# Where SyncE's queue carries the repeat of the step sizes' product and the projection's first loads: two moves in the issue order of a fused scan kernel

## The chip, the cores and the metric

One Trainium2 chip, one core of it. The metric is device time in microseconds (us) of one execution of the whole kernel, lower is better. Times are compared as medians of several runs.

## The reference, cut to what matters

The model runs four images of 64x64 positions and 96 channels through two state-space layers and two attention and feed-forward layers. The time goes into the two state-space layers:

```python
# one state-space layer; K = 4 directions, D = 192 channels, N = 16 states, L = 4096
xz = x @ in_proj_w.T;  xi, z = split(xz)
xc = silu(depthwise_conv3x3(xi) + conv_b)
xs = four orders of the same xc            # layer 0: rows, columns, both backwards; layer 1: windows of 1, 2, 4, 8
dts, Bs, Cs = split(einsum(xs, x_proj_w));  delta = softplus(einsum(dts, dt_w) + dt_b)
def step(h, inp):                          # 4096 times
    h = exp(dt_t[..., None] * A) * h + (dt_t * u_t)[..., None] * B_t[:, :, None, :]
    y = einsum('bkdn,bkn->bkd', h, C_t)
y = sum of the four directions' y, each put back in image order, plus Ds * xs
y = layernorm(y) * silu(z);  x = x + y @ out_proj_w.T
```

## The kernel before, in words

There are eight scans (four images times two layers), in the order image 0 layer 0, image 1 layer 0, image 0 layer 1, image 1 layer 1, and the same for images 2 and 3. I number them 0 to 7. A scan has 16 steps (four directions times four stretches of 1024 positions), 128 steps in all. A step has 24 tiles. A tile is 128 partitions (32 channels times 4 states) by 1024 positions, and its work is spread over the engines like this:

- TensorE fills a PSUM slot with B, repeated over partitions (fill, L1071).
- DVE multiplies it by the product of step size and input, which lies in the buffer `dur` (inp, L1572), and runs the recurrence (states, L1587; L1583 for the two tiles of every eight whose input GpSimd prepares, L1707).
- ScalarE makes the decays from the step sizes in the buffer `dtr` (decay, L1336).
- GpSimd multiplies the states by C, which lies in `crep` (product, L1693). The ring of states has three buffers, so scan n of DVE waits until the product n - 3 is done.
- TensorE sums over the states (reduce2, L1084), ScalarE evicts (collect), SyncE stores (store_y, L770).

`dtr`, `dur`, `crep` and `brep` hold each channel's row repeated over partitions. The repeating is done by DMA: load_dt (L753) and load_du (L762) issue two transfers of 512 KB for each group of eight tiles (three groups, g = 0 to 2, in a step), load_c (L739) one for each q = 0 to 3, used from tile 2q of the step on, and load_b (L744) one, used by GpSimd right after the step's first product. Every DMA of the kernel is issued by SyncE, on one queue, in the order of its program. An instruction that waits there holds all that is behind it.

SyncE's loop over the tiles i = 0 to 23 of step w sets that order. At i = 0 come group 1 of `dtr` and `dur` and `crep` q = 2, at i = 2 q = 3, at i = 8 group 2 of `dtr` and `dur`, and for the next step, w + 1, group 0 of `dtr` at i = 18, group 0 of `dur` and `crep` q = 0 at i = 20, `brep` at i = 21 and `crep` q = 1 at i = 22. The product itself, step size times input, is GpSimd's (delta_u, L1684): its first half, the only one that group 0 needs, is made in tile 17 after the tile's own product. load_du waits for it (du_g), and for the scans that still read the buffer (scan_v).

Beside the scan each engine advances a side program by two half tiles (ticks) a tile, with `next(side)`. From the fifteenth tick of scan s on (tick 14, tile 7; LEAD = 14), it is the projection of scan s - 1 (post): eight chunks of 512 positions, started every 39 ticks. A chunk adds up five inputs of 2 x 192 KB each (SUMS: directions 1, 3, 0 and 2 from `y_d`, then the layer's input from `u_d`), on TensorE in ticks s = 0, 2, 4, 8 and 10 of the chunk (L914), normalises, multiplies by the gate z (load at s = 23, product on GpSimd at s = 29, L1659), projects and adds to the image `xb` at s = 38 (L1489). The first chunk's ticks begin 8 ticks after the post's start (X_LEAD). post_load (L612) issues the inputs: the fifth of a chunk at s = 2, the next chunk's four at s = 12, 4, 31 and 37. For layer 0 directions 1 and 3 are read across the columns, in pieces of 8 elements, which makes 6144 pieces of 32 bytes in each transfer. Scans 1, 2, 5 and 6 have such a projection beside them; scans 3, 4 and 7 have one of layer 1, whose loads are all in long rows. load_x (L586) loads the whole image, 1.5 MB, into `xb`. After the post comes the next conv (pre) or an attention layer (attn), each on the same ticks, then nothing.

Of the kernel before, what the change touches and what calls it, by code (L numbers as in the profile page):

```python
# [238 lines left out]
def follow(*sides):  # L239
    for side in sides:  # L240
        yield from side


def build_program(nc, a, out):
# [6 lines left out]
    def dram(name, shape):  # L251
        return nc.dram_tensor(name, shape, F32, kind="Internal").ap()
# [4 lines left out]
    x_d = dram("x_d", [nb, CH, L])  # L257
# [4 lines left out]
    with ctx:  # L262
# [6 lines left out]
        def after(e, s, n):  # L269
            if n > 0:  # L270
                e.wait_ge(s, n)
# [72 lines left out]
        ykt = [v[0:CH, r, :].rearrange("p (h t) -> p h t", h=2) for v in (hs, dec, us) for r in range(3)]  # L344
# [25 lines left out]
        def lane(c, overlapped):  # L370
            return lanes[0 if overlapped else c % LANES]
# [22 lines left out]
        def sum_buffer(m, n, overlapped):  # L394

            if overlapped:
                i = n % 5
                r = i % 4
                return yk[r], yk_in[r], 32 * (2 * m + i // 4 + 1 if r == 0 else m + 1)
            t, r = divmod(n, len(ykt))
            return ykt[r], ykt_in[r], 32 * (t + 1)
# [4 lines left out]
        def chunk(c):  # L411
            return xb[:, 1 + ROWS * c:1 + ROWS * (c + 1), 1:1 + SIDE]

        def rows(v):
            return v.rearrange("p (r w) -> p r w", w=SIDE)
# [62 lines left out]
        def beside(jobs, stages, overlapped):  # L478


            if overlapped:
                for _ in range(LEAD):
                    yield
            for kind, n in jobs:
                yield from stages[kind](n, overlapped)
# [11 lines left out]
        def post_lead(overlapped):  # L497
            return X_LEAD if overlapped else 0

        def post_every(overlapped):  # L500
            return POST_EVERY if overlapped else POST_LANES
# [7 lines left out]
        def post_ticks(overlapped):  # L509
            return post_every(overlapped) * (C8 - 1) + 39  # L510
# [7 lines left out]
        def landed(m, c, one, of_lane, size, overlapped):  # L518


            return (one, size * (m + 1)) if overlapped else (of_lane[c % LANES], size * (c // LANES + 1))
# [17 lines left out]
        def _(sp):  # L539
            n = 0  # L540
# [45 lines left out]
            def load_x(done, src):  # L586
                after(sp, cu_p, C8 * UNITS * done.pre)
                after(sp, x_out, 16 * done.saves)
                after(sp, o_out, 16 * done.outs)
                sp.wait_ge(set_g, 1)  # L590
                sp.dma_start(xb[:, 1:1 + SIDE, 1:1 + SIDE], rows(src)).then_inc(x_in, 16)
# [20 lines left out]
            def post_load(j, n, overlapped):  # L612
                l = order[j][1]
                c, i = divmod(n, 5)
                m = C8 * before["post", j].post + c
                if not overlapped:
                    after(sp, yt_v, (n - len(ykt)) // 5 + 1)
                elif i == 2:
                    after(sp, pg_g, m)
                elif i == 3:  # L620
                    after(sp, pj_p, m)
                else:
                    after(sp, sm_p, 5 * m + (0, -3, 0, 0, 1)[i])
                buf, arrived, _ = sum_buffer(m, n, overlapped)
                for h in range(2):
                    ch = slice(CH * h, CH * (h + 1))
                    k = SUMS[i]
                    if k == K:
                        src, dst = u_d[j][ch, B * c:B * (c + 1)], buf[:, h, :]
                    elif l == 0 and k % 2 == 1:  # L630
                        src = y_d[j, k][ch, :].rearrange("p (w r) -> p w r", r=SIDE)[:, :, ROWS * c:ROWS * (c + 1)]
                        dst = buf[:, h, :].rearrange("p (w r) -> p w r", r=ROWS)
                    else:
                        src, dst = y_d[j, k][ch, B * c:B * (c + 1)], buf[:, h, :]
                    sp.dma_start(dst, src).then_inc(arrived, 16)

            def post(j, overlapped):
                b, l = order[j]
                done = before["post", j]
                sp.wait_ge(y_out, 32 * NG * STEPS * (j + 1))  # L640
                after(sp, uz_out, 32 * C8 * done.pre)
                after(sp, fy_a, C8 * done.attn)
                if not overlapped:
                    sp.wait_ge(scan_v, W * NT)
                    sp.wait_ge(red_p, W * NP)
                after(sp, fx_g, C8 * done.attn)
                for n in range(4 if overlapped else len(ykt)):
                    post_load(j, n, overlapped)
                load_x(done, a["x"][b] if l == 0 else x_d[b])
                for _ in range(post_lead(overlapped)):  # L650
                    yield
                for tick in range(post_ticks(overlapped)):
                    for c in range(C8):
                        s = tick - post_every(overlapped) * c
                        m = C8 * done.post + c
                        if overlapped and s == 2:
                            post_load(j, 5 * c + 4, True)
                        if overlapped and s in (12, 4, 31, 37) and c + 1 < C8:
                            post_load(j, 5 * (c + 1) + (12, 4, 31, 37).index(s), True)
                        if not overlapped and s == 12:  # L660
                            for n in range(5 * c + len(ykt), min(5 * (c + 1) + len(ykt), 5 * C8)):
                                post_load(j, n, False)
                        if s == 23:
                            sp.wait_ge(pv_p, m + 1)
                            arrived, _ = landed(m, c, zq_in, zqt_in, 32, overlapped)
                            for h in range(2):
                                sp.dma_start(lane(c, overlapped).zq[:, h, :], z_d[j][CH * h:CH * (h + 1), B * c:B * (c + 1)]).then_inc(arrived, 16)
                        if s == 38 and done.saved:
                            sp.wait_ge(px_v, m + 1)
                            sp.dma_start(rows(x_d[b])[:, ROWS * c:ROWS * (c + 1), :], chunk(c)).then_inc(x_out, 16)  # L670
                    yield
# [117 lines left out]
            for w in range(W):  # L789
                if w % STEPS == 0:  # L790
                    side = beside(plan[w // STEPS + 1], stages, True)
                    if w == 0:
                        side = follow(head, side)
                if w % STEPS == STEPS - 1:
                    run(side)
                for i in range(NT):
                    if i == 0:
                        load_dt(1, w)
                        load_du(1, w)
                        if w:  # L800
                            load_c(NQ - 2, w)
                    if i == 2:
                        load_c(NQ - 1, w)
                    if i == 1:
                        if w + 1 < W and late(w + 1):
                            load_u(w + 1)
                    if i == 6 and w + 2 < W and not late(w + 2):
                        load_u(w + 2)
                    if i == 4 and w:
                        store_y(2, w - 1)  # L810
                    if i == 8:
                        load_dt(2, w)
                        load_du(2, w)
                    if i == 12:
                        store_y(0, w)
                    if i == 20:
                        store_y(1, w)
                    if w + 1 < W:
                        if i == (8 if late(w + 1) else 0):
                            store_c(0, w + 1)  # L820
                        if i == (13 if late(w + 1) else 10):
                            store_c(1, w + 1)
                        if i == 18:
                            load_dt(0, w + 1)
                        if i == 20:
                            load_du(0, w + 1)
                        if i == 21:
                            load_b(w + 1)
                        if i in (20, 22):
                            load_c((i - 20) // 2, w + 1)  # L830
                    next(side, None)
                    next(side, None)
# [982 lines left out]
```

## Time and profile before

| | |
|---|---|
| median of 3 runs | 11373.29 us (11363.34 to 11389.22) |
| the profiled execution | 11397.64 us, of which span 11395.9 us |
| DVE busy | 10173.2 us (89%) |
| GpSimd (POOL) busy | 9736.9 us (85%) |
| TensorE busy | 8819.1 us (77%) |
| DMA queue of SyncE | 64.3% of 16 engines' span |

The span is that of one profiled execution; its own time lies 24.4 us above the median. The profile gives for each engine its instructions, how long it sat idle before one, and whose work ended that idle time. SyncE's rows show when a DMA was issued and how long SyncE was held by issuing it.

### The profile page before, as it was taken

How to read it: one execution, taken by the hardware profiler on the slowest of the kernel's cores; microseconds unless marked ns; L12 is line 12 of the kernel's file. 1: busy time of each engine (PE TensorE's matmuls, PEld its weight loads, DVE VectorE, ACT ScalarE, POOL GpSimd, SP SyncE). 2: the span in 40 equal slices, each digit the busy share in tenths (PEclk: the TensorE clock that was granted, in tenths of full speed). 3: DMA queues.
4: the chain of work that ended last, by engine and by line, in shares of the span. 5: the costliest groups of instructions: out<-in, count | busy, mean ns of one | idle time of the engine just before them, and what ended most of it. 6: DMA issues, size and time to landing. Idle time of an engine off the chain costs nothing.

```text
span 11395.9 us, 94804 instructions
## 1 busy us (share of the span) xinstructions
PE 8819.1 (77%) x26272; PEld 2206.4 (19%) x26272; DVE 10173.2 (89%) x6087; ACT 6991.9 (61%) x10714; POOL 9736.9 (85%) x4231
## 2 busy tenths in 40 slices
PE   7876677876778777769777787888688876777767
PEld 2211111211112111212112121122111221122213
DVE  4899998999889999989999998899988999999973
ACT  5665555665556556677565765566755666667644
POOL 4899988899888999989988888888988889998860
PEclk9865577865779568769777787788677876777766
DMA  4666689566875566656776668956687566665550
GB/s 113 141 150 132 134 155 157 152 135 142 158 158 151 132 157 162 151 130 148 169 157 152 133 140 157 158 149 137 137 155 161 136 152 142 159 163 120 125 138 11
DMA packets 1779117, 1627.04 MB, mean 143 GB/s; under 512 B 1323598, under 2 KB 1324912, under 8 KB 1778588
## 3 DMA queue, kind: packets, MB, share of 16 engines
q1 hardware_dynamic: 1778588, 1620.97, 64.3%
q8 instruction: 212, 3.47, 0.1%
q14 instruction: 317, 2.60, 0.1%
HBM read 623.22 MB, written 192.15 MB: 72 GB/s over the span
## 4 chain that ended last, share of the span: by engine, by line
DVE 24%; issue 22%; PE 19%; POOL 18%; ACT 8%; DMA 4%; SPq 3%; DVEq 0%; POOLq 0%; ACTq 0%
POOL pr L1693 13%; DVE hs L1587 10%; DVE ps L1572 9%; DVE hs L1583 4%; PE ps L1084 3%; PE ps L1071 3%; PE ps L879 2%; PE ps L914 2%; PE ps L1062 2%; DMA dur<-us 2%; ACT dec L1336 2%; POOL dur L1707 2%; POOL bup L1707 2%; PE ps L1046 2%; POOL us L1684 1%
## 5 line engine op out<-in xcount | busy, mean ns | idle before, releaser
L1693 POOL TENSOR_TENSOR pr<-hs,crep 128x1024 f32<-128x1024 f32 x3072 | 7184.6, 2355 | 1175.9 <-DVE hs L1587 510.9
L1587 DVE TENSOR_TENSOR_SCAN hs<-dec,carry,ps 128x1024 f32<-128x1024 f32 x1728 | 4054.6, 2346 | 237.6 <-POOL pr L1693 13.4
L1071 PE MATMUL ps<-sbc,selb 96*128 96x512 bf16 x4608 | 1844.0, 492 | 1921.3 <-DVE hs L1587 1310.8
L1572 DVE TENSOR_TENSOR ps<-ps,dur 128x1024 f32<-128x1024 f32 x2304 | 2789.2, 1211 | 436.0 <-PE ps L1071 233.0
L1336 ACT ACTIVATE dec<-dtr,ac 128x1024 f32<-128x1024 f32 x2304 | 2611.0, 1137 | 486.5 <-DVE hs L1587 459.0
L1084 PE MATMUL ps<-pr,red 128*32 128x512 f32 x12288 | 2287.5, 827 | 19.7 <-POOL pr L1693 13.3
L1343 ACT ACTIVATE carry<-hs 128x1 f32<-128x1 f32 x2304 | 457.1, 199 | 2452.5 <-DVE hs L1587 2282.9
L1587 DVE TENSOR_TENSOR_SCAN hs<-dec,zero,ps 128x1024 f32<-128x1024 f32 x576 | 1351.5, 2346 | 72.2 <-ACT dec L1336 1.4
L879 PE MATMUL ps<-xb,tapw 96*96 96x512 f32 x2304 | 1176.8, 632 | 31.1 <-ACT sd L1168 28.5
L1071 PEld LDWEIGHTS ps<-sbc,selb 96*128 96x128 bf16 x4608 | 374.5, 108 | 4058.9 <-DVE hs L1587 2412.3
L1336 ACT ACTIVATE ps<-dtr,ac 128x1024 f32<-128x1024 f32 x768 | 848.6, 1105 | 421.8 <-DVE hs L1587 421.6
L1707 POOL TENSOR_TENSOR dur<-dur,brep 128x1024 f32<-128x1024 f32 x384 | 907.5, 2363 | 2.5 <-DVE ps L1572 2.3
L1707 POOL TENSOR_TENSOR bup<-dur,brep 128x1024 f32<-128x1024 f32 x384 | 905.4, 2358 | 2.3 <-DMA brep<-bc_d 2.3
L1062 PE MATMUL ps<-xdf,tapw 6*96 6x512 f32 x1024 | 777.9, 849 | 50.7 <-ACT de L1311 26.4
L1046 PE MATMUL ps<-us,xp 96*102 96x512 f32 x1024 | 687.6, 808 | 46.1 <-ACT us L1289 24.8
L1583 DVE TENSOR_TENSOR_SCAN hs<-ps,carry,bup 128x1024 f32<-128x1024 f32 x288 | 671.2, 2331 | 57.9 <-issue 30.9
L1684 POOL TENSOR_TENSOR us<-us,de 96x1024 f32<-96x1024 f32 x256 | 603.1, 2356 | 125.3 <-ACT de L1320 125.3
L1583 DVE TENSOR_TENSOR_SCAN hs<-ps,carry,dur 128x1024 f32<-128x1024 f32 x288 | 670.4, 2328 | 13.9 <-ACT ps L1336 7.8
L914 PE MATMUL ps<-sd,eye 96*96 96x512 f32 x896 | 610.0, 799 | 5.2 <-DMA sd<-y_d 3.2
L1084 PEld LDWEIGHTS ps<-pr,red 128*32 128x32 f32 x12288 | 276.7, 124 | 1164.7 <-issue 889.4
L879 PEld LDWEIGHTS ps<-xb,tapw 96*96 96x96 f32 x2304 | 356.6, 169 | 743.4 <-issue 677.7
L1303 ACT ACTIVATE sbc<-ps 96x512 bf16<-96x512 f32 x768 | 443.7, 578 | 16.1 <-PE ps L1052 16.1
(228 smaller groups left out, 7622.2 us busy)
## 6 DMA issues: line engine op xcount, KB each, us to landing
dtr<-de SPq DMA_DIRECT2D x768, 512.0 KB, 8.1
dur<-us SPq DMA_DIRECT2D x768, 512.0 KB, 7.9
crep<-bc_d SPq DMA_DIRECT2D x512, 512.0 KB, 7.3
ust<-u_d SPq DMA_DIRECT2D x256, 384.0 KB, 6.1
y_d<-yst SPq DMA_DIRECT2D x768, 128.0 KB, 2.4
sd<-y_d SPq DMA_DIRECT2D x448, 192.0 KB, 4.6
brep<-bc_d SPq DMA_DIRECT2D x128, 512.0 KB, 7.2
u_d<-sd SPq DMA_DIRECT2D x64, 384.0 KB, 3.1
```

Of the source, the lines that this page charges most:

```text
L879: mm = pe.matmul(bank, tap[:, t, h * CH:(h + 1) * CH], xb[:, c * ROWS + t // 3:c * ROWS + t // 3 + ROWS, t % 3:t % 3 + SIDE], start=(t == ...
L914: mm = pe.matmul(ps[0:CH, bank + h, :], eye[:, :] if k < K else dg[:, l, h, :], v, start=(i == 0), stop=(i == K))
L1046: mm = pe.matmul(ps[0:XROWS, PB, :], xp[:, l, h, k, :], us[:, half(h, w), B * hf:B * (hf + 1)], start=(h == 0), stop=(h == 1))
L1062: pe.matmul(ps[0:CH, PB, :], dtw[:, order[s][1], k, h * CH:(h + 1) * CH], xdf[XD:XROWS, :], start=True, stop=True, tile_position=(XD, 0)). ...
L1071: mm = pe.matmul(ps[:, SLOT + 2 * (n % RS) + hf, :], selb[:, i % GT // 2, :], sbc[:, w % 2, B * hf:B * (hf + 1)], start=True, stop=True)
L1084: mm = pe.matmul(ps[32 * strip:32 * strip + 32, YB, :], red[:, :], pr[:, (2 * m + j) % RP, B * hf:B * (hf + 1)], start=(q == 0), stop=(q = ...
L1336: act.activation(to, dtr[:, 2 * (G % 2) + i % 2, :], ACT.Exp, scale=ac[:, order[s][1], k, i:i + 1]).then_inc(exp_a, 1)
L1572: dve.tensor_tensor(slot(n), slot(n), dur[:, 2 * (G % 2) + i % 2, :], ALU.mult).then_inc(bu_v, 1)
L1583: dve.tensor_tensor_scan(hs[:, n % RH, :], slot(n), bup[:, :] if i % 2 else dur[:, 2 * (G % 2), :], init, ALU.mult, ALU.add).then_inc(scan ...
L1587: dve.tensor_tensor_scan(hs[:, n % RH, :], dec[:, others(n) % RD, :], slot(n), init, ALU.mult, ALU.add).then_inc(scan_v, 1)
L1693: pool.tensor_tensor(pr[:, n % RP, :], hs[:, n % RH, :], crep[:, q, :], ALU.mult).then_inc(prod_g, 1)
L1707: pool.tensor_tensor(to, v, brep[:, :], ALU.mult).then_inc(bup_g, 1)
```

## The change

Three edits in SyncE's program; no other engine's program and no computation changes.

1. load_du(0, w + 1), the repeat of the product for the next step's first group, is issued at i = 18, right behind load_dt(0, w + 1), instead of at i = 20. The side program's ticks 36 to 39 and store_y(1, w) stood between the two places.
2. In the overlapped post the first chunk's four sum inputs (eight DMAs) are no longer issued all at the post's start. They go out in its ticks 0, 2, 4 and 6, so in tiles 7, 8, 9 and 10 of the scan's first step; the group 2 loads of `dtr` and `dur` at i = 8 come between the first and the second.
3. The image's load of the overlapped post moves from right behind those eight to tick 16 behind the lead of 8, which is tick 38 of the step, tile 19: behind load_dt(0), load_du(0), ahead of store_y(1), load_c(0), load_b and load_c(1).

The last post, which runs after all scans, keeps its order.

```diff
-                for n in range(4 if overlapped else len(ykt)):
-                    post_load(j, n, overlapped)
-                load_x(done, a["x"][b] if l == 0 else x_d[b])
-                for _ in range(post_lead(overlapped)):
+                if not overlapped:
+                    for n in range(len(ykt)):
+                        post_load(j, n, False)
+                    load_x(done, a["x"][b] if l == 0 else x_d[b])
+                for tick in range(post_lead(overlapped)):
+                    if tick % 2 == 0:
+                        post_load(j, tick // 2, True)
                     yield
                 for tick in range(post_ticks(overlapped)):
                     for c in range(C8):
...
                         if overlapped and s == 2:
                             post_load(j, 5 * c + 4, True)
+                        if overlapped and tick == 16 and c == 0:
+                            load_x(done, a["x"][b] if l == 0 else x_d[b])
...
                         if i == 18:
                             load_dt(0, w + 1)
-                        if i == 20:
                             load_du(0, w + 1)
```

## Rows read from the trace of the kernel before

**Rows 1.** The page, busy us, share of the span and count of each engine

```profile
PE 8819.1 (77%) x26272; PEld 2206.4 (19%) x26272; DVE 10173.2 (89%) x6087; ACT 6991.9 (61%) x10714; POOL 9736.9 (85%) x4231
```

**Rows 2.** Windows: us, busy of PE, PEld, DVE, ACT, POOL, granted clock, DMA share, GB/s

```profile
650.00:1370.00 720.00, 485.55 (x1398) 83.40 (x1397) 696.29 (x386) 404.15 (x590) 681.21 (x294) 0.58 0.63 137
1470.00:1545.00 75.00, 54.15 (x157) 12.35 (x155) 62.26 (x37) 41.66 (x64) 61.67 (x27) 0.75 1.00 141
1713.00:1810.00 97.00, 76.08 (x217) 17.37 (x215) 78.03 (x45) 49.84 (x55) 81.68 (x36) 0.79 0.94 150
```

**Rows 3.** Waits over the whole span: total us, times, longest

```profile
DVE ps L1572 <- DMA dur<-us: 201.2, 29, 101.6
...
POOL pr L1693 <- DMA crep<-bc_d: 46.7, 6, 10.3
```

**Rows 4.** Timeline of DVE, five waits for dur: start, us, [idle before]

```profile
1508.10 1.23 DVE L1572 TENSOR_TENSOR ps<-ps,dur 128x1024 f32<-128x1024 f32 x1 [3.82 <-DMA dur<-us]
...
1541.51 1.23 DVE L1572 TENSOR_TENSOR ps<-ps,dur 128x1024 f32<-128x1024 f32 x1 [7.19 <-DMA dur<-us]
...
1810.29 1.23 DVE L1572 TENSOR_TENSOR ps<-ps,dur 128x1024 f32<-128x1024 f32 x1 [6.30 <-DMA dur<-us]
...
1900.41 1.23 DVE L1572 TENSOR_TENSOR ps<-ps,dur 128x1024 f32<-128x1024 f32 x1 [2.88 <-DMA dur<-us]
...
7819.75 1.23 DVE L1572 TENSOR_TENSOR ps<-ps,dur 128x1024 f32<-128x1024 f32 x1 [3.29 <-DMA dur<-us]
```

**Rows 5.** Timeline of SyncE, scan 1, step 0: start, us it was held

```profile
1468.56 16.41 SPq L635 DMA_DIRECT2D sd<-y_d  x7
1485.07 0.58 SPq L591 DMA_DIRECT2D xb<-in_x  x1
1485.75 10.92 SPq L753 DMA_DIRECT2D dtr<-de  x2
...
1532.53 1.26 SPq L762 DMA_DIRECT2D dur<-us  x2
1533.88 3.83 SPq L739 DMA_DIRECT2D crep<-bc_d  x1
```

**Rows 6.** Issues of crep: first the one of 1533.88, then that of 1828.05

```profile
DMA to landing us min/median/max: 9.4/9.4/9.4
...
DMA to landing us min/median/max: 7.1/7.1/7.1
```

**Rows 7.** Timeline of SyncE and POOL in a step with nothing beside it

```profile
889.58 1.26 SPq L762 DMA_DIRECT2D dur<-us  x2
...
886.49 2.35 POOL L1684 TENSOR_TENSOR us<-us,de 96x1024 f32<-96x1024 f32 x1
```

**Rows 8.** Timeline, scan 1, step 1: POOL's first product, DVE's eighth scan

```profile
1546.26 2.35 POOL L1693 TENSOR_TENSOR pr<-hs,crep 128x1024 f32<-128x1024 f32 x1 [6.56 <-DVE hs L1587]
...
1568.70 2.32 DVE L1583 TENSOR_TENSOR_SCAN hs<-ps,carry,bup 128x1024 f32<-128x1024 f32 x1
```

**Rows 9.** Timeline, scan 1, step 4: SyncE's third crep, POOL's fifth to seventh product

```profile
1828.05 1.74 SPq L739 DMA_DIRECT2D crep<-bc_d  x1
...
1835.28 6.97 POOL L1693 TENSOR_TENSOR pr<-hs,crep 128x1024 f32<-128x1024 f32 x3 [5.70 <-issue]
```

**Rows 10.** Timeline, scan 3, steps 0 and 1: SyncE's crep, POOL's product

```profile
4214.85 3.84 SPq L739 DMA_DIRECT2D crep<-bc_d  x1
...
4230.54 1.67 SPq L739 DMA_DIRECT2D crep<-bc_d  x1
...
4246.87 9.30 POOL L1693 TENSOR_TENSOR pr<-hs,crep 128x1024 f32<-128x1024 f32 x4
```

**Rows 11.** Timeline, scan 3, step 3: input load, delta_u, its user on PE

```profile
4456.23 2.84 SPq L635 DMA_DIRECT2D sd<-u_d  x2
...
4460.22 2.36 POOL L1684 TENSOR_TENSOR us<-us,de 96x1024 f32<-96x1024 f32 x1
...
4468.40 1.96 PE L914 MATMUL ps<-sd,dg 96*96 96x512 f32 x4
```

## The prediction

> **What bounds the kernel now.** I read the page first: DVE is busy 89% of the span and GpSimd 85% [rows 1]. The windows say where the rest is lost. With nothing beside the scan DVE works 696.3 of 720 us and the DMA engines are busy 0.63 of the time; in the first step of scan 1, where the projection starts, DVE works 62.3 of 75 us and the DMA share is 1.00, and it is 0.94 in step 3 [rows 2]. Of DVE's waits 201.2 us are for `dur`, in 29 waits; the one of 101.6 is the start of the kernel, so 99.6 us in 28 waits can be at stake [rows 3]. They are not spread evenly. I sorted all of them by step, and one wait of each kind stands as an example [rows 4]:
> - first step of scans 1, 2, 5 and 6, the ones with a layer-0 projection: 3.82 before tile 16 and 7.19 before the next step; over the four scans such pairs come to 11.0, 11.0, 9.7 and 11.2, in all 42.9 us;
> - the end of step 3 of the same scans, 6.30 and three like it, together 21.6;
> - the end of step 4, 2.88 and three like it, 12.4;
> - the end of step 10 of scans 5 and 6, 3.29 and 3.64, 6.9;
> - some ten of 0.7 to 2.8 us, mostly the end of step 2, the rest.
>
> SyncE's own timeline tells why. At 1468.56 seven of the eight sum loads hold it for 16.41 us, then comes the image, and the next transfer (dtr, two DMAs) holds it for 10.92; the loads of group 0 for the next step go out only at 1532.53 [rows 5]. An issue costs 0.6 us when the queue is short (1.26 for two there), so the long ones are the queue being full. The image thus occupies it for some 10.3 us (10.92 less one issue of 0.6).
>
> **Part 1, the earlier dur.** In a quiet step it changes nothing: dur goes out at 889.58 while the product it carries is finished at 886.49 + 2.35 = 888.84 [rows 7]. The gain is 0.7 us of lead that nobody waits for. So about 90 of 128 steps are unmoved. Where the queue is full, the two transfers swap places with what stood between, but the work in the queue is the same. What comes after dur (`crep` q = 0, `brep`, q = 1, the next dtr and dur, q = 2) lands no sooner. So the next limit is GpSimd's `crep`, and I price each kind by it.
>
> End of step 3 (21.6 us of DVE waits): nothing comes back. In that case q = 2 goes out at 1828.05 and lands 7.1 later, at 1835.2 [rows 6, 9]; GpSimd, which has waited 5.70 for it, starts its fifth product at 1835.28 [rows 9], and the ring of three lets DVE's eighth scan go only behind that product. DVE would start its step 6.3 earlier and lose it eight tiles later. The input loads that now stand behind dur put about 1 us of transfer into the full stretch. Bounds: -1.5 to +6 a step; I take -1, since the limiting landing is in the trace. Four steps: -4.
>
> End of step 4 (12.4 us): no crep wait follows, so most comes back. The bound below is 0 (a column load behind dur goes out later and pushes `crep`), above 12.4. I take 8. End of step 10 (6.9 us): dtr is stuck behind an image load, dur can follow it at once; bounds 3 and 6.9, I take 6. The scattered ones are followed in scans 1, 2, 5 and 6 by a crep wait of about 10 us, of which the longest is 10.3 [rows 3], so I take 1 for them together, between 0 and 12.
>
> **Part 2, the spread loads.** With one pair of column loads ahead of dtr and dur of group 2 instead of eight DMAs and the image, these go out in tile 8 and, 9.4 us or less from issue to landing like the crep of rows 6, are there long before tile 16. The 3.82 goes. The sum loads now land when their users are due within about a microsecond; I charge 0.4 a scan.
>
> The 7.19 before the next step goes only in part. All that stood ahead of `crep` q = 0 still does, the image included, and the queue is full from 1468 to 1545 [rows 2], so q = 0 lands at 1533.88 + 9.4 = 1543.3 [rows 5, 6] as before, or a little sooner. GpSimd, which started at 1546.26 after DVE's wait [rows 8], can start then: 3.0 us, which is the bound below. DVE may be three tiles ahead of it, though, so its loss is less. From 1543.3 GpSimd needs five products and two inputs at 2.35 each, 16.5 us, to 1559.8; that releases DVE's eighth scan, which began at 1568.70 [rows 8]. That is 8.9, against 11.0 if all comes back. Less 0.4, 8.5 in each of the four scans: +34, with 12 and 43 as ends.
>
> The image moves into the end of step 0 of scans 3, 4 and 7 too, where no wait for dur stood. There it puts 10.3 us ahead of `crep`. q = 0 went out at 4214.85 and would land around 4224; q = 2 went out at 4230.54, and lands near 4238.5, while its product starts at 4246.87 [rows 10]: 8.4 us in hand. Ten more eat that, and GpSimd's first products start 2 to 4 us late. Ends 0 and 6 us a scan, I take 2.5: -7.5. The Trainium skill, page DMA: Bandwidth & Descriptors, section Anatomy of one DMA, would put such a transfer at 2.0 us plus its bytes by 436 GB/s, 5.6 us for 1.5 MB as an estimate; the trace disagrees with its 10.3 of queue, and by the page's price these 7.5 us would be nearly nothing and the sum about 11334.
>
> **The new wait.** At i = 18 SyncE now stands until the product is made. Behind it are the side ticks 36 to 39 and the store of y. The store's buffer is wanted seven tiles later, so it hides. In step 2 or 3 of a projection the tick holds the fifth input. In scan 3 it went out at 4456.23; the product ends at 4460.22 + 2.36 = 4462.6, so it goes out near 4463.9 and lands behind dur, about 4472, while TensorE wants it at 4468.40 [rows 11]. TensorE stands 3 us, DVE's next fill is due 4 to 6 us later, so 0 to 3 of it shows; 1 for each of three scans, -3. The conv's stores at those ticks delay ScalarE by up to 2 us in some four places: -2, between 0 and -6. Gate loads go out later too, but their product on GpSimd is 10 us away: 0.
>
> **Sum.** 34 - 4 + 8 + 6 + 1 - 7.5 - 3 - 2 = 32.5 us. Against the profiled execution that is 11397.64 - 32.5 = 11365; it lies 24.4 above the median, so for the median 11373.29 - 32.5 = 11341 us. A measurement can tell 0.2% from no change, 23 us here.
>
> **Rivals.**
> 1. *The full queue gives it all back.* The DMA share of 0.94 to 1.00 in the stretches at stake [rows 2] and the landing that pins DVE [rows 9] speak for it. Then the first steps give only GpSimd's 3.0 each, 12; the end of step 4 gives 4 and of step 10 gives 3; and -4, -7.5, -3 and -2 stay: 2.5 us, so 11371. By the Trainium skill, page DMA: Bandwidth & Descriptors, section Queues, rings and completion order, transfers of one issuing engine share one ring on each of the same DMA engines and are consumed in ring order, so reordering makes no room; the trace agrees as far as its share of 1.00 goes.
> 2. *Everything waited for comes back.* If shorter column bursts also let `crep` land sooner, all 99.6 us of DVE's waits go, and 11274 is reached. Against it: POOL's 46.7 us of waits for crep [rows 3] lie right behind them.
> 3. *Slower: the image pushes `crep` off.* Its 10.3 us now stand between dur and q = 0 in seven first steps. It decides where GpSimd has less in hand than that. In scans 3, 4 and 7, 8.4 us are in hand for q = 2 but only 1 or 2 for q = 0; if DVE pays 8 in each, 24 are lost. If in the other four q = 0 also lands later than 1543.3, by 5 us, 3 us of loss each takes the place of the 8.5 gained, -12. With 4 and 3 gained at steps 4 and 10 and -4 for step 3, -3 and -2, that is 38 us more, 11411; half of it gives 11392.
>
> **How the numbers follow.** Forecast 0.53, rival 1 0.29, rival 2 0.10, rival 3 0.08. The forecast's own range is 11318 to 11362, from the ends of its largest term (12 or 43 in place of 34) and a few us of the others. Eight in ten: down to 11295, which leaves most of rival 2 out, and up to 11386, which takes in rival 1 and part of rival 3. Faster by over 0.2% means under 11350.5: about 0.46 of the forecast's 0.53, rival 2, and 0.05 of rival 1, 0.61. Slower by over 0.2% means over 11396: 0.05. Between them 0.34.
>
> **What would show it.** In the changed trace DVE's waits for `dur` beside layer-0 projections are gone or below 1 us; if they are not, dur is late for its product. GpSimd's waits for `crep` grow from 46.7 us to about 80, above all at q = 0 of step 1; if they don't, rival 2 holds. Step 0 of scan 1 is 8 to 9 us shorter than before, and step 3 as long as before, 97 us (the window of rows 2). In scan 3 the fifth product of step 1 starts 2 to 3 us later against its step's first tile. I am wrong if the gain of step 3 is kept, if the image's 10.3 us costs nothing in scans 3, 4 and 7, or if the steps with nothing beside them change in length.

## The result, and the profile after

The changed kernel takes 11412.5 us (median of 5 runs, 11410.21 to 11451.97) against 11371.33 for the kernel before (5 runs, 11363.34 to 11389.22): ratio 1.0043 [1.003, 1.0056], so it is slower by 0.43%. Measured a second time it came out at 1.0032 [1.0019, 1.0044]. The forecast was 11341. The two profiled executions differ less, 11397.64 and 11411.21 us, because the one of before lies 26 us above its median. The two profiles of the changed kernel differ by 20 us, so step lengths below are compared as sums over several steps, where possible from two profiles of each kernel.

In the changed kernel load_du is L767, load_dt L758, load_c L744, load_b L749, store_y L775, GpSimd's product L1697, DVE's inp L1576.

The page of the changed kernel, busy us of each engine, answers to [rows 1]: as busy as before.

```profile
PE 8871.1 (78%) x26272; PEld 2220.9 (19%) x26272; DVE 10173.8 (89%) x6087; ACT 6994.2 (61%) x10714; POOL 9742.8 (85%) x4231
```

Its windows, the same stretches as in [rows 2] (us, busy of PE, PEld, DVE, ACT, POOL, granted clock, DMA share, GB/s):

```profile
650.00:1370.00 720.00, 488.03 (x1399) 83.53 (x1398) 696.31 (x387) 404.38 (x590) 681.50 (x295) 0.57 0.62 137
1470.00:1545.00 75.00, 58.16 (x166) 12.98 (x169) 68.83 (x41) 46.10 (x71) 61.97 (x27) 0.70 0.90 124
1713.00:1810.00 97.00, 79.87 (x218) 18.82 (x217) 81.23 (x48) 50.34 (x55) 80.22 (x36) 0.74 0.93 149
```

The quiet stretch is the same (DVE 696.3 in both). In the first step of scan 1 DVE works 68.8 of 75 us in place of 62.3, as wanted, and GpSimd no more than before.

Its waits (total us, times, longest) answer to [rows 3]:

```profile
DVE ps L1576 <- DMA dur<-us: 111.1, 7, 101.5
...
POOL pr L1697 <- DMA crep<-bc_d: 76.1, 10, 10.1
...
ACT sd L1172 <- DMA z_d<-sd: 55.1, 13, 6.9
```

DVE's waits for `dur` are nearly gone: less the start of the kernel, 9.6 us are left of 99.6, most of it 1.5 to 2.2 us at the end of step 0 of scans 1, 2, 5 and 6. GpSimd's for `crep` grew from 46.7 to 76.1 (62.8 in the second profile). The third line is one that the prediction never listed: ScalarE waits until a conv store to `z_d` has left its buffer, 18.0 us in 8 waits before, 55.1 in 13 now.

Where the time went, by steps. A step's length is the time from DVE's first product with `dur` in it to that in the next, added up over the scans named. "Before" is the mean of two profiles, of the kernel before and of the experiment e8, which differs from it in step 7 alone (for step 7 only the kernel before is taken); "changed" is the mean of its two profiles. Two profiles of one kernel differ by up to 6.2 us in the first row and by 4.4 in the others with steps 3 or 4, but by 0.1 in step 7 of the changed kernel. So -3.5 can't be told from nothing, and +18.4 can.

| steps | before | changed | difference |
|---|---|---|---|
| 0 and 1 of scans 1, 2, 5, 6 | 705.3 | 701.8 | -3.5 |
| 3 and 4 of scans 1, 2, 5, 6 | 741.7 | 732.2 | -9.5 |
| 5 of scans 1, 2, 5, 6 | 334.4 | 339.7 | +5.3 |
| **7 of scans 1, 2, 5, 6** | 350.9 | 369.4 | **+18.4** |
| 0 and 1 of scans 3, 4, 7 | 485.2 | 492.5 | +7.2 |
| 2 of scans 3, 4, 7 | 258.8 | 250.7 | -8.1 |
| 3 of scans 3, 4, 7 | 250.2 | 257.0 | +6.8 |
| 11 and 12 of scans 3, 4, 7 | 521.5 | 532.2 | +10.7 |
| all others, by step and group of scans none over 3.4 | | | +9.3 |
| sum | | | +36.6 |

So the gains are small, and a loss stands in places where no wait for `dur` had been.

**Step 7** (steps are numbered from 0). SyncE and then ScalarE in step 7 of scan 1, kernel before (start, us, [idle before]):

```profile
2144.63 0.32 SPq L608 DMA_DIRECT2D u_d<-sd  x1
2145.00 0.45 SPq L609 DMA_DIRECT2D z_d<-sd  x1
...
2149.86 1.25 SPq L762 DMA_DIRECT2D dur<-us  x2
...
2154.30 0.68 ACT L1168 ACTIVATE sd<-ps,cb 96x512 f32<-96x512 f32 x1 [1.54 <-PE ps L879]
```

The same in the changed kernel, with DVE's scan that waits for ScalarE:

```profile
2140.64 1.19 SPq L767 DMA_DIRECT2D dur<-us  x2
2141.87 3.94 SPq L608 DMA_DIRECT2D u_d<-sd  x1
2145.86 2.28 SPq L609 DMA_DIRECT2D z_d<-sd  x1
...
2153.61 0.68 ACT L1172 ACTIVATE sd<-ps,cb 96x512 f32<-96x512 f32 x1 [6.88 <-DMA z_d<-sd]
...
2155.34 2.35 DVE L1587 TENSOR_TENSOR_SCAN hs<-ps,carry,bup 128x1024 f32<-128x1024 f32 x1 [3.90 <-ACT ps L1340]
```

And the time from issue to landing of the store to `z_d`, before:

```profile
DMA to landing us min/median/max: 3.9/3.9/3.9
```

and changed:

```profile
DMA to landing us min/median/max: 7.7/7.7/7.7
```

Counted from the first product of step 7 (2070.4 before, 2064.7 changed), the store to `u_d` is issued at 74.2 and at 77.1: that is the wait for the product. Its issue then holds SyncE 3.9 us in place of 0.3, and the store to `z_d` lands 7.7 after its issue in place of 3.9, with the megabyte of `dur` and the other store ahead of it in the queue. It lands at 78.5 before and at 88.8 now. ScalarE's next eviction into that buffer stands 6.88 us, the decays behind it come late, and DVE stands 3.90. All four scans show it: 4.6 us longer each in the first profile, to 0.1.

### The profile page after: what moved, and what is told of

Read it like the earlier page. It is cut to its first block and busy times, and to the rows that moved or that the text cites. A ratio compares the mean times of both kernels' runs of the same rounds, so it can differ in the third digit from the quotient of the medians.

```text
span 11409.4 us, 94804 instructions
## 1 busy us (share of the span) xinstructions
PE 8871.1 (78%) x26272; PEld 2220.9 (19%) x26272; DVE 10173.8 (89%) x6087; ACT 6994.2 (61%) x10714; POOL 9742.8 (85%) x4231
## 5 line engine op out<-in xcount | busy, mean ns | idle before, releaser
L1697 POOL TENSOR_TENSOR pr<-hs,crep 128x1024 f32<-128x1024 f32 x3072 | 7187.3, 2356 | 1193.1 <-DVE hs L1591 500.4
L1576 DVE TENSOR_TENSOR ps<-ps,dur 128x1024 f32<-128x1024 f32 x2304 | 2787.8, 1210 | 382.4 <-PE ps L1075 269.2
```

The costliest lines, as they stand in the source:

```text
L1576: dve.tensor_tensor(slot(n), slot(n), dur[:, 2 * (G % 2) + i % 2, :], ALU.mult).then_inc(bu_v, 1)
L1697: pool.tensor_tensor(pr[:, n % RP, :], hs[:, n % RH, :], crep[:, q, :], ALU.mult).then_inc(prod_g, 1)
```

## The experiments

Step lengths are in us. Each group of four ran on one chip with the kernel before beside it. The first group asks which part does what.

**e1_dur18**: part 1 alone, the loads as before.

```diff
                         if i == 18:
                             load_dt(0, w + 1)
-                        if i == 20:
                             load_du(0, w + 1)
```

> Part 1 alone: dur for the next step goes out in the nineteenth tile, the projection's loads and the image stay in one burst as before. Theory A (the new wait for the product holds SyncE, and with it the side program's ticks 36 to 39: fifth sum input in step 3, conv stores in step 7): slower than before by 25 to 50 us, and step 7 of scans 1, 2, 5 and 6 about 4.6 us longer, as in the changed kernel. Theory B (the image ahead of crep is what costs): this kernel is faster than before by 10 to 30 us. Theory C (the DMA queue is full, order changes nothing): within 10 us of before.

Measured: 1.002 [1.001, 1.003]. Steps 0 and 1 of scans 1, 2, 5, 6 take 692.7 (705.3 before), steps 3 and 4 take 730.3 (741.7), but step 7 takes 369.9 (350.9) and step 3 of scans 3, 4, 7 257.6 (250.2). Part 1 is a loss by itself, 21 us by the medians, less than the 25 to 50 of theory A. In the first steps it gives 12.6 of the 34 us that were forecast there, more than both parts together. DVE's waits for `dur` in steps 0 and 1 of the four scans are 39.5 us there, hardly less than the 42.9 of before.

**e2_spread_image_late**: part 2 alone, with `dur` in tile 20.

```diff
                         if i == 18:
                             load_dt(0, w + 1)
+                        if i == 20:
                             load_du(0, w + 1)
```

(against the changed kernel)

> Part 2 alone: sum loads spread, image in tile 19, dur in tile 20 as before. Theory A: 15 to 35 us faster than before, since step 0 of scans 1, 2, 5 and 6 still gets 5 us shorter and nothing is held. Theory B: slower than before by 10 us or more, since the image now stands ahead of dur too (it is issued in tile 19, dur in tile 20). Theory C: within 10 us.

Measured: 1.0048 [1.0035, 1.0061], the highest ratio of all, as theory B had it. SyncE and DVE at the end of step 0 of scan 1:

```profile
1517.64 4.03 SPq L591 DMA_DIRECT2D xb<-in_x  x1
1521.71 12.43 SPq L775 DMA_DIRECT2D y_d<-yst  x2
1534.24 1.26 SPq L767 DMA_DIRECT2D dur<-us  x2
...
1543.42 1.23 DVE L1577 TENSOR_TENSOR ps<-ps,dur 128x1024 f32<-128x1024 f32 x1 [13.78 <-DMA dur<-us]
```

The image holds the next issue, the y store, for 12.43 us; `dur` goes out behind both and DVE stands 13.78. Step 0 becomes 5 to 8 us longer in scans 1, 2, 5, 6 and 5 to 11 in 3, 4 and 7. In the changed kernel `dur` is ahead of the image and escapes this; what is behind does not.

**e3_spread_image_early**: the loads spread, the image in half tile 7 of the lead, `dur` in tile 20.

```diff
-                for n in range(4 if overlapped else len(ykt)):
-                    post_load(j, n, overlapped)
-                load_x(done, a["x"][b] if l == 0 else x_d[b])
-                for _ in range(post_lead(overlapped)):
+                for tick in range(post_lead(overlapped)):
+                    if tick % 2 == 0:
+                        post_load(j, tick // 2, True)
+                    if tick == 7:
+                        load_x(done, a["x"][b] if l == 0 else x_d[b])
                     yield
```

> Sum loads spread over the opening half tiles, but the image right behind them (half tile 7 of the lead, tile 10) and dur in tile 20 as before. Only the burst is undone. Theory A and theory B both: faster than before by 15 us (the 3.8 to 5.2 us wait of group 2 in four scans), crep q = 0 not later than before. Theory C: within 5 us of before, the wait returns as a longer one before the next step.

Measured: 0.9992 [0.9983, 1.0]. Step 0 stays as it was, 358.7 against 359.1 over the four scans. DVE's two waits of [rows 4] in scan 1 are now

```profile
1502.13 1.23 DVE L1577 TENSOR_TENSOR ps<-ps,dur 128x1024 f32<-128x1024 f32 x1 [3.86 <-PE ps L1076]
...
1535.40 1.23 DVE L1577 TENSOR_TENSOR ps<-ps,dur 128x1024 f32<-128x1024 f32 x1 [7.06 <-DMA dur<-us]
```

The one before tile 16 (3.82 for `dur`) has only changed its name: `dur` is there and DVE stands 3.86 for TensorE's fill. The one before the next step is as it was (7.19). The expected gain of 15 us in step 0 did not come. So it is in every kernel with the loads spread: in step 0 of the four scans DVE waits 15.7 to 20.8 us for TensorE's fill, and 0 to 4.2 in those with the loads in one burst.

**e4_dur20**: `dur` stays in tile 20, but goes ahead of the y store.

```diff
                     if i == 20:
+                        if w + 1 < W:
+                            load_du(0, w + 1)
                         store_y(1, w)
...
-                        if i == 20:
-                            load_du(0, w + 1)
```

> dur for the next step stays in tile 20 but goes ahead of the store of y instead of behind it: it passes only the two stores, and no side tick is held (the product is done by then). Theory A: faster than before by 5 to 20 us, step 7 of scans 1, 2, 5, 6 as before. Theory B: the same, 10 to 30 us faster. Theory C: within 5 us of before.

Measured: 0.9986 [0.9977, 0.9996]. In step 7 of scan 1 (SyncE, then ScalarE) the conv's stores go first and ScalarE waits for TensorE, not for a store:

```profile
2131.78 0.32 SPq L608 DMA_DIRECT2D u_d<-sd  x1
2132.14 0.45 SPq L609 DMA_DIRECT2D z_d<-sd  x1
2133.79 1.21 SPq L762 DMA_DIRECT2D dur<-us  x2
...
2156.76 0.69 ACT L1168 ACTIVATE sd<-ps,cb 96x512 f32<-96x512 f32 x1 [0.96 <-PE ps L879]
```

Step 7 takes 349.4 over the four scans, step 3 of scans 3, 4, 7 takes 250.1, as before; steps 3 and 4 of the four scans take 733.0 (741.7). The loss is gone and more than half of the gain kept. In step 7 the early place had bought no lead at all: `dur` is issued 72.7 to 76.3 us into the step in the four scans here, and 72.5 to 76.5 in e1, since both wait for the same product. Only what stands behind it differs. In step 3, where the queue is full, e1 is some 4 us earlier (76.4 to 79.2 against 81.5 to 82.9).

The second group tests the account of step 7, the image's place, and whether the parts add.

**e8_dur18_step7_only**: the kernel before, tile 18 in 8 of 128 steps.

```diff
                             load_dt(0, w + 1)
-                        if i == 20:
+                        if i == (18 if w % STEPS == 7 else 20):
                             load_du(0, w + 1)
```

> The kernel before, with the product's repeat in tile 18 in the seventh step of each scan alone (8 of 128 steps), in tile 20 elsewhere. Theory A: step 7 of scans 1, 2, 5 and 6 longer by 4.6 us each, +18 us, ratio 1.0016, with ScalarE waiting up to 7 us for the gate's store; all other steps as before. Rival: the seventh step is long because of what the earlier steps left (the side work shifted), then it stays within 1 us of before and the ratio at 1.000.

Measured: 1.0024 [1.0015, 1.0033]. Step 7 of scans 1, 2, 5, 6 takes 369.7, 18.8 more than before, the others as before. SyncE, ScalarE and DVE in scan 1:

```profile
2139.01 1.19 SPq L762 DMA_DIRECT2D dur<-us  x2
2140.24 3.95 SPq L608 DMA_DIRECT2D u_d<-sd  x1
...
2151.81 0.68 ACT L1168 ACTIVATE sd<-ps,cb 96x512 f32<-96x512 f32 x1 [6.70 <-DMA z_d<-sd]
...
2153.53 2.35 DVE L1583 TENSOR_TENSOR_SCAN hs<-ps,carry,bup 128x1024 f32<-128x1024 f32 x1 [3.73 <-ACT ps L1336]
```

The move in this one step gives the whole pattern, and the rival, that earlier steps leave step 7 long, is out. Its 18.8 us are 0.17%, in the lower part of the measured interval.

**e9_after_image_early**: the changed kernel with the image back in half tile 7 of the lead.

```diff
+                    if tick == 7:
+                        load_x(done, a["x"][b] if l == 0 else x_d[b])
                     yield
...
-                        if overlapped and tick == 16 and c == 0:
-                            load_x(done, a["x"][b] if l == 0 else x_d[b])
```

> The changed kernel with the image back in the lead (half tile 7 of the post), so that part 1 and the spread loads stay and only the image's place is undone. Theory A and B together: parts add, so e1 (1.002) times e3 (0.9992), about 1.001, 35 us under the changed kernel; step 0 of scans 1, 2, 5 and 6 as in the kernel before, step 7 still 4.6 us longer. If the image's place is innocent, it stays at 1.004.

Measured: 1.0015 [1.0006, 1.0024]. Steps 0 and 1 take 693.8 in scans 1, 2, 5, 6 (changed 701.8) and 482.5 in 3, 4, 7 (changed 492.5): 18 us by the late image. The landing of step 1's first `crep` shows it in all seven scans: counted from the start of step 0, q = 0 lands at 91.7 (before), 90.7 (here) and 97.0 us (changed) on average in scans 1, 2, 5 and 6, and at 79.8, 79.3 and 88.9 in 3, 4 and 7. The expectation that step 0 stays as before did not hold: it is 349.9 (359.1), since `dur` in tile 18 shortens it here too.

**e7_after_image_tile23**: the changed kernel with the image in tile 23, behind `crep` q = 0, `brep` and q = 1.

```diff
-                        if overlapped and tick == 16 and c == 0:
+                        if overlapped and tick == 25 and c == 0:
```

> The changed kernel with one thing moved: the image goes out in tile 23 of the first step, behind store_y(1), crep q=0, brep and crep q=1, in place of tile 19. Theory B (the image ahead of the store and of crep takes back what the first steps gained): steps 0 and 1 of scans 1, 2, 5 and 6 together 3 to 6 us shorter than in the changed kernel, those of scans 3, 4 and 7 by 2 to 4, 20 to 30 us in all, so ratio near 1.002; what is left over 1.000 is the wait in tile 18. Theory C: the image only pushes q=2 and q=3 off in place of q=0, and the time stays at 1.004.

Measured: 1.0036 [1.0024, 1.0049], where theory B expected 1.002 and theory C 1.004. SyncE in scan 1:

```profile
1532.65 0.56 SPq L744 DMA_DIRECT2D crep<-bc_d  x1
...
1535.94 0.66 SPq L591 DMA_DIRECT2D xb<-in_x  x1
1536.70 12.67 SPq L758 DMA_DIRECT2D dtr<-de  x2
```

`crep` q = 0 goes out at 1532.65, not 1543.07 (this profile runs 1.2 us ahead there), and steps 0 and 1 of the four scans take 694.2, as with the image early. But the image now holds group 1 of `dtr` for 12.67 us, and in scans 3, 4 and 7 the same two steps take 495.7, 3 more than changed and 13 more than in e9. GpSimd's first product of step 1 is back at its old place there, 5.4 to 6.7 us into the step (9.1 to 10.8 changed), but its fifth, which needs q = 2, starts at 26.3 to 28.0 (25.3 to 26.9 changed, 21.6 to 22.8 before). So theory B came in scans 1, 2, 5 and 6, and theory C in 3, 4 and 7: the image pushes off q = 2 in place of q = 0. It is not the place ahead of q = 0 alone that costs, but the stretch at the turn of the step.

**e6_spread_early_dur20**: e3 and e4 together.

> The two halves that did no harm alone, put together: the four sum loads spread over the lead, the image in half tile 7 of it (ahead of everything of the next step), and the product's repeat in tile 20 but ahead of store_y(1). Theory A (the wait in tile 18 is what costs, the order of the loads gives some us): 0.9992 times 0.9986, about 0.998, some 20 us under the kernel before; the seventh steps of scans 1, 2, 5 and 6 as long as before. Theory C (the queue is full, so no order of it gives anything): within 0.1% of before, and the waits for crep grow by what those for dur lose.

Measured: 0.9992 [0.9983, 1.0001]. Step 7 is as before (349.2). The two small gains do not add.

The third group puts tile 18 only where the first group showed a gain, with the loads in three orders.

**a2_changed_again**: the changed kernel once more.

> The changed kernel itself, on the chip and beside the runs of before of the three below. All theories: the ratio of the first measurement, 1.0043, within its interval of 1.003 to 1.0056.

Measured: 1.0032 [1.0019, 1.0044].

**e10_dur18_steps0to3**: loads as before; `dur` in tile 18 in steps 0 to 3 of scans 1, 2, 5, 6, in tile 20 ahead of the y store elsewhere.

```diff
+            def first_steps(w):
+                return w % STEPS < 4 and w // STEPS in (1, 2, 5, 6)
...
                             load_dt(0, w + 1)
-                        if i == 20:
-                            load_du(0, w + 1)
+                            if first_steps(w):
+                                load_du(0, w + 1)
...
                     if i == 20:
+                        if w + 1 < W and not first_steps(w):
+                            load_du(0, w + 1)
                         store_y(1, w)
```

> Part 1 only where it did good: the product's repeat in tile 18 in steps 0 to 3 of scans 1, 2, 5 and 6, elsewhere in tile 20 ahead of store_y(1); loads of the projection and image as before. Theory A (tile 18 gains in these steps, 14 us in step 3 and about 6 in step 0, and loses in step 7 and in scans 3 and 7): step 7 as before, step 3 of the four scans 14 us shorter together, ratio 0.997 to 0.998, under the 0.9986 of tile 20 everywhere. Rival (what is gained in steps 0 and 3 is given back in steps 1, 4 and 5): 0.9986 or above.

Measured: 1.0 [0.9991, 1.0008]. Step 3 of the four scans takes 366.8 (383.3 before), but step 4 takes 370.1 (358.4): of 16.5 us won, 11.7 come back one step later. The rival named there holds: no gain of tile 18 over tile 20 (e4) shows, even where it shortens a step most.

**e11_steps0to3_spread_early**: the same with the loads of e3.

> The kernel of the run before this with the four sum loads spread over the lead and the image at its half tile 7. If spreading helps once the wait is placed well, another 0.05 to 0.1% under it; if the spread is worth nothing (0.9992 alone, and it added nothing to tile 20), the same within 0.1%.

Measured: 0.9994 [0.9986, 1.0003], the same as e10 within the intervals.

**e12_steps0to3_spread_late**: the same with the loads as changed.

> The changed kernel with tile 18 kept in steps 0 to 3 of scans 1, 2, 5 and 6 alone, so that part 2 stands as changed but the wait is gone from step 7 and the later ones. Theory B (the late image loses by itself, in step 1 of all seven scans and, where dur is in tile 20, in step 0 of scans 3, 4 and 7): 0.2 to 0.4% above the run with the image early, so ratio 1.000 to 1.002. If part 2 only lost through part 1's wait, the same as that run, 0.998.

Measured: 1.0011 [1.0002, 1.002], 0.17% above e11, where 0.2 to 0.4 was expected. Step 0 of scans 3, 4, 7 takes 256.6 (237.6 in e11), since `dur` is in tile 20 there, behind the image:

```profile
4202.80 3.50 SPq L591 DMA_DIRECT2D xb<-x_d  x1
4208.96 9.98 SPq L767 DMA_DIRECT2D dur<-us  x2
...
4227.45 1.23 DVE L1583 TENSOR_TENSOR ps<-ps,dur 128x1024 f32<-128x1024 f32 x1 [5.46 <-DMA dur<-us]
```

Step 7 takes 350.1, so the changed kernel without its wait in the later steps is back from 1.0032 to 1.0011 on the same chip, in spite of these 19 us.

## Why the prediction was wrong

The sign was wrong: 32.5 us of gain were forecast, and 36 to 49 lost (0.32 and 0.43% of 11380). Of the 69 us between forecast and table 30.5 lie in the first steps and 20 in the two terms of the new wait; both steps of the prediction failed, and the first steps are the larger. Rival 3 had the time, 11411, by luck. Its mechanism was seen: it let `crep` q = 0 land 5 us later in scans 1, 2, 5 and 6, and it does so by 5.3 on average. But it put 36 us of loss on that, where the rows of the first steps lose 3.7 net, and 5 on the new wait.

**The new wait, -5, cost 25: this gave the loss.** I priced it at 3 us for the fifth input and "by up to 2 us in some four places: -2, between 0 and -6" for the conv's stores. The stores alone cost 18.4, the fifth input 6.8 (step 3 of scans 3, 4 and 7 takes 254.8 to 261.3 us in the five profiles with tile 18 in every step, 246.3 to 252.9 in the other nine). I had only looked at the wait. In the changed kernel those DMAs also stand behind the two transfers of `dur`, and the store's landing moved by 10.3 us, of which the wait is 2.9, the hold of the store ahead 3.6 and the longer way to landing 3.8. e8 shows the store's part alone, and e4 that nothing of it is left once the side ticks go ahead of `dur`. For the input, SyncE, TensorE and DVE in step 3 of scan 3 of the changed kernel:

```profile
4462.46 1.19 SPq L767 DMA_DIRECT2D dur<-us  x2
4463.69 6.01 SPq L635 DMA_DIRECT2D sd<-u_d  x2
...
4472.98 3.73 PE L918 MATMUL ps<-sd,dg 96*96 96x512 f32 x4 [3.85 <-DMA sd<-u_d]
...
4477.66 1.23 DVE L1576 TENSOR_TENSOR ps<-ps,dur 128x1024 f32<-128x1024 f32 x1 [3.11 <-PE ps L1075]
```

The times were nearly right (the input's issue at 4463.9 and its landing at 4472 foretold, 3 us of waiting on TensorE), but DVE pays 3.11 of the 3.85, where I let 1 show.

A third place was not priced at all: the attention's inputs (`t_d`) on the same ticks in step 12 of scan 7. TensorE waits 7.7 us for them there (8.1 in the second profile), 1.8 before. Step 12 of scan 7 is 96.6 to 97.1 us in the five profiles read that have tile 18 in every step (after, its repeat, e1, e7, e9) and 91.3 to 91.4 in the other nine. Scan 3's step 11 scatters from 91.2 to 101.5 with and without the wait, so of the 10.7 in the table some 5.3 are shown.

**The first steps, +34, gave 3.5: the larger miss.** In steps 0 and 1 of the four scans, as the mean of two profiles of each kernel, DVE's waits for `dur` fell from 43.7 to 9.1 us. But those for TensorE's fill rose from 21.6 to 37.2, and 15.2 us of waits for GpSimd's product (the ring of three) are new. So two limits that I had priced at next to nothing took the gain. For the ring, the step that failed is "All that stood ahead of `crep` q = 0 still does ..., so q = 0 lands at 1533.88 + 9.4 = 1543.3 ... as before, or a little sooner". SyncE in scan 1 of the changed kernel, which answers to [rows 5]:

```profile
1501.09 16.16 SPq L635 DMA_DIRECT2D sd<-y_d  x4
1517.35 4.01 SPq L758 DMA_DIRECT2D dtr<-de  x2
1521.46 6.91 SPq L767 DMA_DIRECT2D dur<-us  x2
1528.46 2.49 SPq L591 DMA_DIRECT2D xb<-in_x  x1
1530.99 11.97 SPq L775 DMA_DIRECT2D y_d<-yst  x2
1543.07 0.57 SPq L744 DMA_DIRECT2D crep<-bc_d  x1
```

The landing of that `crep`, for [rows 6]:

```profile
DMA to landing us min/median/max: 3.8/3.8/3.8
```

q = 0 lands at 1546.9, 3.6 later than before. The work ahead of it is the same, but the queue was not equally full all along. Windows of the changed kernel ahead of it:

```profile
1498.00:1510.00 12.00, 12.00 (x27) 2.76 (x26) 9.17 (x5) 6.91 (x10) 7.49 (x4) 0.81 0.78 95
1510.00:1530.00 20.00, 15.99 (x63) 4.12 (x60) 19.33 (x12) 14.67 (x21) 19.80 (x9) 1.00 0.77 93
```

and of e9, which has the image early:

```profile
1498.00:1510.00 12.00, 12.00 (x26) 2.65 (x25) 9.04 (x6) 6.63 (x11) 7.49 (x5) 0.79 1.00 181
1510.00:1530.00 20.00, 16.54 (x64) 4.26 (x62) 19.33 (x12) 14.67 (x21) 19.81 (x9) 1.00 0.97 86
```

With the image away the DMA engines are 0.78 and 0.77 busy there, with it 1.00 and 0.97: 12 x 0.22 + 20 x 0.20 = 6.6 us of them stand unused, and the 1.5 MB come later on top. What follows on GpSimd and DVE in scan 1, step 1 of the changed kernel, for [rows 8]:

```profile
1547.01 2.35 POOL L1697 TENSOR_TENSOR pr<-hs,crep 128x1024 f32<-128x1024 f32 x1 [7.54 <-DVE hs L1591]
...
1553.92 2.35 POOL L1663 TENSOR_TENSOR sd<-sd 96x1024 f32<-96x1024 f32 x1
...
1549.45 2.35 DVE L1591 TENSOR_TENSOR_SCAN hs<-dec,carry,ps 128x1024 f32<-128x1024 f32 x1 [1.51 <-POOL pr L1697]
...
1565.60 2.35 DVE L1587 TENSOR_TENSOR_SCAN hs<-ps,carry,bup 128x1024 f32<-128x1024 f32 x1
```

GpSimd starts right after the landing (the profile puts its idle time down to DVE's scan, which had long been done). DVE in turn waits behind the ring, here 1.51 us. By my own count of 16.5 us from the landing, 1546.9 gives 1563.4; DVE's eighth scan starts at 1565.60, 3.1 before the old 1568.70, not 8.9. The count had left out one operation: between its second and third product GpSimd also makes the gate's product (L1663), 2.35 us. Eight operations from 1547.01 end at 1565.5. Over the four scans step 0 is 19 us shorter and step 1 is 15 longer.

For the fill: "The 3.82 goes" did not hold. DVE before the same tile 16 in the changed kernel:

```profile
1507.25 1.23 DVE L1576 TENSOR_TENSOR ps<-ps,dur 128x1024 f32<-128x1024 f32 x1 [2.69 <-PE ps L1075]
```

TensorE is busy for all of 1498 to 1510 (12.00 of 12 us in both windows above), much of it with the projection's sums, so its fill comes late too. The wait for `dur` lay over a wait for TensorE, and 1.1 us of 3.82 come back. This part stays with the image early: in e9 DVE waits 36.0 us for the fill in these eight steps, and 17.8 for `dur`, but none for the ring.

**The others.** The image in scans 3, 4 and 7: 7.5 forecast, 7.2 found, and in scan 3 GpSimd's fifth product of step 1 starts 2.5 us later into its step (2 to 3 foretold). The Trainium skill, page DMA: Bandwidth & Descriptors, section Anatomy of one DMA, gives its 2.0 us plus bytes by 436 GB/s as a fit per DMA, measured on DMAs that GpSimd issues; my estimate of 5.6 us from it, for SyncE's load in a full queue, did not fit here either: the issue behind it is held for 11.97, 12.43 and 12.67 us in three kernels. The end of steps 3 and 4: +4 forecast, +9.5 found, of which step 5 takes 5.3 back, so 4.2. The mechanism of step 3 holds; GpSimd's fifth product of step 4 still waits for `crep`, which answers to [rows 9]:

```profile
1832.28 9.28 POOL L1697 TENSOR_TENSOR pr<-hs,crep 128x1024 f32<-128x1024 f32 x4 [9.47 <-DMA crep<-bc_d]
```

and q = 2 lands no sooner, as I had said. The product starts 3.0 us before the old 1835.28, but its step 3 started 3.5 earlier; counted from there q = 2 lands at 121.8 us before and 122.2 now on average over the four scans. The end of step 10 in scans 5 and 6: 6 forecast, 2.8 found, where two profiles of the changed kernel differ by 2.9. Step 2 of scans 3, 4 and 7 gave 8.1 that I had not counted (the waits of 1.4, 1.8 and 1.9 us before the next step, 5.1 of it, are gone), and step 5 of the four scans lost 5.3 whose cause I cannot name.

Right were: no change in the quiet steps, and DVE's waits for `dur` nearly gone. Those for `crep`, at 76.1 ("about 80"), were right in part by luck: they were to grow "above all at q = 0 of step 1", where the profile puts GpSimd's idle time down to DVE, and 28.9 of them are three waits in step 4. Of the other signs, step 0 of scan 1 is 6.9 us shorter (8 to 9 foretold), and its step 3 is not 97 us long as before but 93.8. "I am wrong if the gain of step 3 is kept" came partly true: of the 14.0 us by which step 3 is shorter over the four scans, 4.5 come back in step 4 and 5.3 in step 5.

**How the parts stand.** The wait of tile 18 in the later steps: from e12 (1.0011) to the changed kernel (1.0032), 0.21%, and that is too little, since e12 pays 19 us in step 0 of scans 3, 4 and 7 that the changed kernel does not. The late image: from e9 (1.0015) to the changed kernel (1.0032 and 1.0043), 0.17 to 0.28%; by steps, 18 us, 0.16%. Spreading the loads: nothing that can be told (e3, e11).

No version is faster by more than the 0.2% that this measurement can tell. The best is e4, 0.9986 [0.9977, 0.9996], some 16 us. What stays open: where the 5.3 us of step 5 come from (they are waits of DVE for TensorE's fill and the decays, and e3, which has neither tile 18 nor a late image, is as long there, 338.7), how much of the loss in steps 11 and 12 of scan 3 is the change, and why e10, whose profiled execution has the shortest span (11363.3 us), has no shorter median.

One rival was not tested: TensorE's mean granted clock is 0.734 to 0.740 in the eleven executions of the changed kernel and 0.739 to 0.744 in those of the kernel before, and DVE's waits for TensorE's fill grew. Step 7 is free of it: e8 has 0.740 to 0.745 and loses all the same. For the rest no run tells whether the lower clock costs something by itself or only comes with the longer waits.

## What to carry to other kernels

When an issue is moved forward on a queue, price what it overtakes, not only what it carries: here the overtaken stores paid the wait (2.9 us) and then the hold and the transfer time of what now stood ahead (7.4), and the engine that owns their buffer paid that again. In this kernel the place just behind the last small transfer that something waits for (tile 20, ahead of the y store) was better than the earliest legal one, which went out no sooner in step 7. And a large load that nobody waits for yet was cheapest early, in the stretch where less that was urgent stood behind it; put off to the turn of the step it left the DMA engines partly idle before (6.6 us) and stood ahead of urgent transfers after. When a wait is to be removed, look for the next one underneath: here TensorE's fill and GpSimd's ring stood behind it.

## What the runs showed that I had not expected

A store of 384 KB that lands in 3.9 us where the queue is short takes 7.7 behind one megabyte of repeats and another store, and that other store's issue held the engine for 3.9 us in place of 0.3. In the first steps of scan 1 the image of 1.5 MB is issued in 0.6 us where little stands ahead of it and in up to 4.0 behind other loads, and the row of the issue behind it shows 10.6 to 12.7 us: the hold that a transfer causes stands in the row of what follows it. And a landing can be short because the issue was late: the `crep` of scan 1 lands in 3.8 us after an issue at 1543.07, and in 9.4 after one at 1533.88. The sum of both is what counts.
